# The down projection of batches 1 to 3 as seven block products per pair of chunks

## The chip, the cores and the metric

The kernel runs on one core of one Trainium2 chip. The time is the device time of one execution in microseconds (us). Before the change it is 421.93 us, the median of 3 runs (421.92 to 422.65).

## The reference

Two layers, each added to its input x (4 batches, 512 tokens, 256 features, all float32). The first mixes eight 256x256 weight matrices by eight numbers per batch and applies the mix. The second is a mixture of gated MLPs (256 to 1024 to 256): of eight experts each batch uses the two with the largest softmax weight, and one shared MLP is used by every batch.

```python
def _gemma_mlp(x, gate_w, up_w, down_w):
    g = jnp.einsum('bsh,hi->bsi', x, gate_w)
    u = jnp.einsum('bsh,hi->bsi', x, up_w)
    return jnp.einsum('bsi,ih->bsh', jax.nn.gelu(g, approximate=True) * u, down_w)
...
    masked_w = weight * mask[None, :, :]
    w_bot = jnp.einsum('bg,got->bot', y, masked_w)
    return jnp.einsum('bnt,bot->bno', x, w_bot) + bias
...
x = x + _L0_cond_ref(x, cond_8, L0_cond_weight, L0_cond_mask, L0_cond_bias)
x = x + _L1_cond_ref(x, cond_8, L1_cond_skill_gate, L1_cond_skill_up, L1_cond_skill_down, L1_cond_shared_gate, L1_cond_shared_up, L1_cond_shared_down)
```

## The kernel before

Everything lies feature-major: 128 features on the partitions, the 512 tokens of one batch (T) along the free axis, so the 256 features are two halves (HH). The batches go one after the other; batches 0 to 2 are one loop on every engine, batch 3 (the last) is written out. A batch is 24 **steps**. A step is one chunk of 128 of the 1024 inner features of one MLP: steps 0 to 7 are the shared MLP, 8 to 15 and 16 to 23 the two routed experts.

Each float32 operand is split into a high and a low part of type fp32r (`_hi`, `_lo`), and a product is three matmuls: hi by hi, hi by lo, lo by hi. A step is therefore 12 matmuls for gate and up (`gate_up`, L296 to L328: two projections, two input halves, three parts) and 6 for down (`down`, L330 to L345: two output halves, three parts), each of 128x128 weights over 512 columns. The down products of all 24 steps of a batch add up in one PSUM tile `o_ps`. TensorE's order at step s is `gate_up(s + 2)`, then `down(s)`, and once per batch, at step 13, the 12 matmuls of the next batch's first layer. `g_ps` and `u_ps` have two banks each and change places every step.

The other engines work on one step's data after the other:

- ScalarE: `gelu` from `g_ps` (L444), the high parts of one chunk of routed weights (`ex_hi`, L453, 768 columns: gate, up and down), the high part of h (`h_hi`, L456).
- VectorE: h = gelu times up, times the routing weight in routed steps (`form_h`, L614 to L624, written over `u_ps`), then the low part (`split_h`, L629, reads `u_ps` in PSUM and `h_hi` in SBUF). Between them stand the mixing of the next batch's first-layer weights (L584 to L596) and the low parts of the next batch's input (`x_lo`, L600).
- GpSimd: the low part of one chunk of routed weights per step (`ex_lo`, L721, 768 columns, both inputs in SBUF), in 16 of a batch's 24 steps.
- SyncE starts the loads: one chunk of weights is 384 KB (`raw`).

The order on each engine is written out by hand; engines wait for one another by counted semaphores (`g_done`, `gelu_done`, `h_done`, `h_hi_done`, `h_lo_done`, `w_lo_done`, `down_done`).

Of the kernel before, what the change touches and what calls it, by code (L numbers as in the profile page):

```python
# [22 lines left out]
WARM_UP = 5
L0_STEP = 13


def build(nc, xT, cond, l0_w, l0_mask, experts, shared, outT):
    B, _, HH, T = xT.shape
    G = l0_w.shape[0]
    E, CHUNKS, _, WC = experts.shape  # L30
# [13 lines left out]

    assert RAW_SLOTS == CHUNKS == RING and STEPS % 2 == 0 and STEPS % H_SLOTS == 0 and G == E == 8 and FIRST + SPLIT_LEAD + 1 == CHUNKS

    with ExitStack() as ctx:
# [78 lines left out]
        raw_in = [sem(f"raw_in{i}") for i in range(RAW_SLOTS)]  # L128
# [656 lines left out]
```

## Time and profile before

| | |
|---|---|
| median of 3 runs | 421.93 us (421.92 to 422.65) |
| the profiled execution, its own time | 422.23 us |
| its span (first to last instruction) | 420.1 us |
| TensorE busy (matmul) | 415.3 us, 99% |
| VectorE busy | 189.7 us, 45% |
| ScalarE busy | 184.7 us, 44% |
| GpSimd busy | 140.3 us, 33% |
| TensorE clock granted | 0.999 of full speed |

The page counts for each engine the time in which an instruction runs. Around the span lie 2.1 us of the profiled execution's own time.

### The profile page before, as it was taken

To read this page: it belongs to the slowest core of one execution; us is meant where nothing else is said; L and a number is where in the kernel's file an instruction comes from. 1 tells how busy PE (TensorE), PEld (TensorE's weight loads), DVE (VectorE), ACT (ScalarE), POOL (GpSimd) and SP (SyncE) were. 2 spreads that over 40 slices of the span, in tenths; PEclk is the share of its full clock that TensorE was granted. 3 is DMA by queue.
4 is the path that set the end of the run, shared out by engine and by line. 5 is a ranking of instruction groups with operands and counts; after the bars stand their busy time and mean duration, and the time that the engine had idled before them with its cause. 6 is when DMAs were issued, how large, how long until landed. Compare 5 with 4: busy or idle time off the path is not lost.

```text
span 420.1 us, 5339 instructions
## 1 busy us (share of the span) xinstructions
PE 415.3 (99%) x1827; PEld 342.5 (82%) x1827; DVE 189.7 (45%) x300; ACT 184.7 (44%) x306; POOL 140.3 (33%) x86
## 2 busy tenths in 40 slices
PE   8999999999999999999999999999999999999997
PEld 6778888888888888888888888888888888888886
DVE  3567744353345455444344545524434433333434
ACT  5676454453324545345232554534422445354421
POOL 1566535343001354535100335443300053444500
PEclk9999999999999999999999999999999999999999
DMA  7964332312011323223102132322300123210001
GB/s 272 352 196 158 100 109 79 114 62 89 0 51 49 101 87 107 81 75 111 39 0 101 37 112 75 112 79 71 112 0 0 51 75 113 76 37 0 2 0 50
DMA packets 14849, 35.05 MB, mean 83 GB/s; under 512 B 1650, under 2 KB 3186, under 8 KB 14834
## 3 DMA queue, kind: packets, MB, share of 16 engines
q1 hardware_dynamic: 14544, 34.61, 24.9%
q10 hardware_dynamic: 290, 0.26, 0.2%
q8 instruction: 7, 0.11, 0.1%
q14 instruction: 8, 0.07, 0.0%
HBM read 32.77 MB, written 2.10 MB: 83 GB/s over the span
## 4 chain that ended last, share of the span: by engine, by line
PE 96%; DMA 1%; DVE 1%; SPq 1%; issue 0%; ACT 0%; DVEq 0%
PE o_ps L342 30%; PE g_ps L321 21%; PE u_ps L321 21%; PE u_ps L327 10%; PE g_ps L327 10%; DMA l_raw<-l_w 1%; PE l_ps L286 1%; PE l_ps L291 1%; PE l_ps L270 0%; DVE l_first L560 0%; PE l_ps L357 0%; SPq L188 0%; DVE out_sb L653 0%; PE l_ps L274 0%; SPq L176 0%
## 5 line engine op out<-in xcount | busy, mean ns | idle before, releaser
L721 POOL TENSOR_TENSOR ex_lo<-raw,ex_hi 128x768 fp32r<-128x768 f32 x64 | 123.4, 1929 | 240.7 <-ACT ex_hi L453 240.7
L444 ACT ACTIVATE gelu<-g_ps 128x512 f32<-128x512 f32 x96 | 57.4, 598 | 175.6 <-PE g_ps L327 175.4
L624 DVE SCALAR_TENSOR_TENSOR u_ps<-gelu,route_cur,u_ps 128x512 f32<-128x512 f32 x64 | 48.3, 755 | 125.5 <-ACT gelu L444 125.5
L629 DVE TENSOR_TENSOR h_lo<-u_ps,h_hi 128x512 fp32r<-128x512 f32 x96 | 66.3, 691 | 31.6 <-ACT h_hi L456 30.5
L456 ACT CAST h_hi<-u_ps 128x512 fp32r<-128x512 f32 x96 | 56.4, 588 | 37.1 <-DVE u_ps L619 18.5
L453 ACT CAST ex_hi<-raw 128x768 fp32r<-128x768 f32 x64 | 52.9, 826 | 0.0
L321 PE MATMUL g_ps<-x_hi,ex_hi 128*128 (+1 forms) x128 | 49.8, 389 | 0.0
L321 PE MATMUL g_ps<-x_hi,ex_lo 128*128 (+1 forms) x128 | 49.8, 389 | 0.0
L321 PE MATMUL u_ps<-x_hi,ex_hi 128*128 (+1 forms) x128 | 49.8, 389 | 0.0
L321 PE MATMUL u_ps<-x_hi,ex_lo 128*128 (+1 forms) x128 | 49.8, 389 | 0.0
L342 PE MATMUL o_ps<-h_hi,ex_hi 128*128 128x512 f32 x122 | 47.5, 389 | 0.0
L342 PE MATMUL o_ps<-h_lo,ex_hi 128*128 128x512 f32 x122 | 47.5, 389 | 0.0
L342 PE MATMUL o_ps<-h_hi,ex_lo 128*128 128x512 f32 x122 | 47.5, 389 | 0.0
L619 DVE TENSOR_TENSOR u_ps<-gelu,u_ps 128x512 f32<-128x512 f32 x32 | 22.2, 695 | 43.7 <-ACT gelu L444 43.7
L327 PE MATMUL u_ps<-x_lo,ex_hi 128*128 (+1 forms) x128 | 39.4, 389 | 0.0
L327 PE MATMUL g_ps<-x_lo,ex_hi 128*128 (+1 forms) x128 | 39.4, 389 | 0.0
L321 PEld LDWEIGHTS g_ps<-x_hi,ex_hi 128*128 128x128 f32 x128 | 24.0, 188 | 5.0
L321 PEld LDWEIGHTS u_ps<-x_hi,ex_lo 128*128 128x128 f32 x128 | 24.0, 188 | 5.0
L327 PEld LDWEIGHTS g_ps<-x_lo,ex_hi 128*128 128x128 f32 x128 | 24.0, 188 | 5.0
L321 PEld LDWEIGHTS u_ps<-x_hi,ex_hi 128*128 128x128 f32 x128 | 24.0, 188 | 5.0
L321 PEld LDWEIGHTS g_ps<-x_hi,ex_lo 128*128 128x128 f32 x128 | 24.0, 188 | 5.0
L327 PEld LDWEIGHTS u_ps<-x_lo,ex_hi 128*128 128x128 f32 x128 | 24.0, 188 | 5.0
(119 smaller groups left out, 561.6 us busy)
## 6 DMA issues: line engine op xcount, KB each, us to landing
raw<-experts SPq DMA_DIRECT2D x64, 384.0 KB, 2.9
raw<-shared SPq DMA_DIRECT2D x8, 384.0 KB, 8.2
l_raw<-l_w SPq DMA_DIRECT2D x8, 256.0 KB, 6.0
x_in<-xT SPq DMA_DIRECT2D x8, 256.0 KB, 4.3
outT<-out_sb SPq DMA_DIRECT2D x8, 128.0 KB, 2.0
outT<-out_sb SPq DMA_DIRECT2D x3, 256.0 KB, 2.1
mask<-l_mask SPq DMA_DIRECT2D x2, 128.5 KB, 6.2
outT<-out_sb ACTq DMA_DIRECT2D x2, 128.0 KB, 2.0
```

The lines of the kernel that those rows point to most:

```text
L286: pe.matmul(l0_ps[:, oh], w[:, at:at + P], x_hi[:, th], start=(th == 0 and w is l0_hi), stop=False)
L291: mm = pe.matmul(l0_ps[:, oh], l0_hi[:, at:at + P], x_lo[:, th], start=False, stop=(th == HH - 1))
L321: pe.matmul(ps, w[:, at:at + P], x1_at(x1_hi, b, hh), start=(hh == 0 and w is w_hi), stop=False)
L327: mm = pe.matmul(ps, w_hi[:, at:at + P], x1_at(x1_lo, b, hh), start=False, stop=(hh == HH - 1))
L342: mm = pe.matmul(o_ps[:, oh], w[:, at:at + P], x[:, s % H_SLOTS], start=(s == 0 and i == 0), stop=((closes or s == STEPS - 1) and i == 2))
L444: act.activation(gelu[:, s % 2], g_ps[:, s % 2], ACT.Gelu_apprx_tanh).then_inc(gelu_done, 1)
L453: act.copy(ex_hi[:, j % RING], raw[:, j % RAW_SLOTS]).then_inc(w_hi_done, 1)
L456: act.copy(h_hi[:, s % H_SLOTS], u_ps[:, s % 2]).then_inc(h_hi_done, 1)
L619: dve.tensor_tensor(u_ps[:, s % 2], gelu[:, s % 2], u_ps[:, s % 2], ALU.mult).then_inc(h_done, 1)
L624: dve.scalar_tensor_tensor(u_ps[:, s % 2], gelu[:, s % 2], route_cur[:, k:k + 1], u_ps[:, s % 2], ALU.mult, ALU.mult).then_inc(h_done, 1)
L629: dve.tensor_tensor(h_lo[:, s % H_SLOTS], u_ps[:, s % 2], h_hi[:, s % H_SLOTS].bitcast(F32), ALU.subtract).then_inc(h_lo_done, 1)
L721: pool.tensor_tensor(lo, raw[:, slot], hi.bitcast(F32), ALU.subtract).then_inc(w_lo_done, 1)
```

## The change

The down projection of two chunks (a **pair**, steps 2p and 2p+1) is a product of 2 by 2 blocks: two output halves by two chunks of weights, times two chunks by two halves of the tokens (256 columns, TH). After the change it is done with seven block products in place of eight, as P1 to P7, in 34 pairs: all 12 of batches 1 and 2, and the first 10 of batch 3 (`fast(b, p)`). Batch 0 and the last two pairs of batch 3 stay as they were; batch 0 is now written out too, and batches 1 and 2 are the loop.

- TensorE: a fast pair is 21 matmuls over 256 columns, `products_123` (9) at the even step and `products_4567` (12) at the odd one, in place of 12 over 512. They add up over a batch in seven quarters and halves of banks. `g_ps` is one bank now, the other holds P1, P6 and P7; so the gate matmuls of step s+1 wait until the gelu of step s has read it, and all six gate matmuls stand ahead of the six for up.
- VectorE, per fast pair: the even step's h goes to `h_a` in SBUF (`form_a`); T1 to T4, sums and differences of token halves of the two chunks, are four instructions of 256 columns (`form_t1`, `form_t234`); their low parts are one of 1024 columns (`split_t`), in the next pair's even step; the low parts of h itself are `split_b11` (256 columns, from `h_a`) and `split_b2` (512, from `u_ps`). In the odd steps 7 to 21 of fast pairs VectorE forms S1 to S4 of the next pair but one's routed weights, four instructions of 128x128 (`expert_s`).
- ScalarE: one copy of 1024 columns more per fast pair (`split_t`, high parts), 384 + 512 columns of down weights (`split_d`) and 512 of gate and up per step (`split_gu`) in place of 768.
- GpSimd: the same widths for the low parts. It forms the shared S1 to S4 once, late in batch 0 (`shared_s`, from down weights loaded a second time), and takes the low parts of the next batch's input from VectorE (`split_x`, `split_x1`). Behind batches 1 and 2 it puts the products together with x (`sum_products`, five additions); ScalarE copies the products out of PSUM first, and VectorE adds P4. In batch 3 VectorE adds the products.
- Loads: gate and up (256 KB) and down (128 KB) come apart, in rings of four and two.

```diff
+A11, A12, A22, A21, S1, S2, S3, S4 = 0, 1, 2, 3, 3, 4, 5, 6
+B11, B21, B22, T1, T3, T2, T4 = 0, 1, 2, 3, 4, 5, 6
...
+        h_hi = sb("h_hi", [P, 7 * TH], F32R)
+        h_lo = sb("h_lo", [P, 7 * TH], F32R)
+        t_raw = sb("t_raw", [P, 4 * TH])
+        h_a = sb("h_a", [P, T])
...
-        g_ps = psum("g_ps", [P, 2, T])
...
+        g_ps = psum("g_ps", [P, T])[:]
...
+        P1, P6, P7 = p_ps[:, 0, 0:TH], p_ps[:, 1, 0:TH], p_ps[:, 1, TH:T]
+        P2, P3, P4, P5 = o_ps[:, 0, 0:TH], o_ps[:, 0, TH:T], o_ps[:, 1, 0:TH], o_ps[:, 1, TH:T]
...
+        def fast(b, p):
+            return not at_first(b) and not (at_last(b) and p >= LAST_FAST)
...
+                pe.wait_ge(gelu_done, n)
+                project(g_ps, w_hi, w_lo, GATE, b).then_inc(g_done, 1)
...
+            def product(ps, wt, ht, blk, hf, first, last):
+                for i, (w, h) in enumerate(((0, 0), (0, 1), (1, 0))):
+                    mm = pe.matmul(ps, block_of(wt[w], blk), half_of((h_hi, h_lo)[h], hf), start=(first and i == 0), stop=(last and i == 2))
...
+            def products_123(b, p):
+                wait_d(b, p)
+                pe.wait_ge(h_lo_done, STEPS * b + 2 * p + 2)
...
+                product(P1, wt, None, A11, B11, first, last)
+                product(P2, wt, None, A12, B21, first, False)
+                product(P3, wt, None, S4, B22, False, last).then_inc(down_done, 1)
...
+            def products_4567(b, p):
+                pe.wait_ge(t_lo_done, pair_count(b, p) + 1)
...
+                product(P6, wt, None, S2, T2, first, False)
+                product(P7, wt, None, S3, T3, False, last)
+                product(P4, wt, None, A22, T4, first, False)
+                product(P5, wt, None, S1, T1, False, last).then_inc(down_done, 1)
...
+                if fast(b, PAIRS + q):
+                    act.copy(ed_hi[:, q % RING_D, 0:3 * P], raw_d[:, slot, 0:3 * P]).then_inc(d_hi_done, 1)
+                    act.wait_ge(s_raw_done, 4 * s_count(b, q) + 4)
+                    act.copy(ed_hi[:, q % RING_D, S1 * P:7 * P], s_raw[:]).then_inc(s_hi_done, 1)
...
+            def split_t(b, p):
+                act.wait_ge(t_done, 4 * pair_count(b, p) + 4)
+                act.wait_ge(down_done, STEPS * b + 2 * p)
+                act.copy(h_hi[:, T1 * TH:7 * TH], t_raw[:]).then_inc(t_hi_done, 1)
...
+            def form_t1(b, p):
+                if not (isinstance(b, int) and b == 1 and p == 0):
+                    dve.wait_ge(t_lo_done, pair_count(b, p))
+                dve.wait_ge(h_done, STEPS * b + 2 * p + 1)
+                dve.tensor_tensor(t_part(T1), h_a[:, TH:T], h_a[:, 0:TH], ALU.subtract).then_inc(t_done, 1)
...
+            def form_t234(b, p):
+                dve.tensor_tensor(t_part(T3), u_ps[:, 1, TH:T], h_a[:, TH:T], ALU.subtract).then_inc(t_done, 1)
+                dve.wait_ge(t_done, 4 * pair_count(b, p) + 1)
+                dve.tensor_tensor(t_part(T2), u_ps[:, 1, TH:T], t_part(T1), ALU.subtract).then_inc(t_done, 1)
+                dve.wait_ge(t_done, 4 * pair_count(b, p) + 3)
+                dve.tensor_tensor(t_part(T4), u_ps[:, 1, 0:TH], t_part(T2), ALU.subtract).then_inc(t_done, 1)
...
+            def split_b11(b, p):
+                dve.wait_ge(h_hi_done, STEPS * b + 2 * p + 1)
+                dve.tensor_tensor(h_lo[:, 0:TH], h_a[:, 0:TH], h_hi[:, 0:TH].bitcast(F32), ALU.subtract).then_inc(h_lo_done, 1)
...
+            def split_b2(b, p):
+                dve.wait_ge(h_hi_done, STEPS * b + 2 * p + 2)
+                at = slice(B21 * TH, (B22 + 1) * TH)
+                dve.tensor_tensor(h_lo[:, at], u_ps[:, 1], h_hi[:, at].bitcast(F32), ALU.subtract).then_inc(h_lo_done, 1)
...
+            def split_t(b, p):
+                dve.wait_ge(t_hi_done, pair_count(b, p) + 1)
+                at = slice(T1 * TH, 7 * TH)
+                dve.tensor_tensor(h_lo[:, at], t_raw[:], h_hi[:, at].bitcast(F32), ALU.subtract).then_inc(t_lo_done, 1)
...
+            def expert_s(b, q):
...
+                dve.tensor_tensor(out(S1), blk(A21), blk(A22), ALU.add).then_inc(s_raw_done, 1)
+                dve.tensor_tensor(out(S3), blk(A11), blk(A21), ALU.subtract).then_inc(s_raw_done, 1)
+                dve.wait_ge(s_raw_done, n + 1)
+                dve.tensor_tensor(out(S2), out(S1), blk(A11), ALU.subtract).then_inc(s_raw_done, 1)
+                dve.wait_ge(s_raw_done, n + 3)
+                dve.tensor_tensor(out(S4), blk(A12), out(S2), ALU.subtract).then_inc(s_raw_done, 1)
...
+            def step(b, s, with_next):
+                p = s // 2
+                if not fast(b, p):
+                    form_h(b, s)
+                    if s % 2 == 0 and s > 0 and fast(b, p - 1):
+                        split_t(b, p - 1)
+                    beside(b, s, with_next)
+                    split_h(b, s)
+                elif s % 2 == 0:
+                    form_a(b, p)
+                    if p > 0 and fast(b, p - 1):
+                        split_t(b, p - 1)
+                    beside(b, s, with_next)
+                    form_t1(b, p)
+                    split_b11(b, p)
+                else:
                     form_h(b, s)
                     beside(b, s, with_next)
-                    split_h(b, s)
+                    split_b2(b, p)
+                    form_t234(b, p)
+                q = (s - CHUNKS + 1) // 2
+                if not at_first(b) and s % 2 and 0 <= q < EPR and fast(b, PAIRS + q):
+                    expert_s(b, q)
...
+            def split_d(b, q):
+                pool.wait_ge(d_hi_done, PAIRS + EPR * b + q + 1)
+                slot = d_slot(b, q)
+                if fast(b, PAIRS + q):
+                    pool.tensor_tensor(ed_lo[:, q % RING_D, 0:3 * P], raw_d[:, slot, 0:3 * P], ed_hi[:, q % RING_D, 0:3 * P].bitcast(F32), ALU.subtract)
+                    pool.wait_ge(s_hi_done, s_count(b, q) + 1)
+                    pool.tensor_tensor(ed_lo[:, q % RING_D, S1 * P:7 * P], s_raw[:], ed_hi[:, q % RING_D, S1 * P:7 * P].bitcast(F32), ALU.subtract).then_inc(d_lo_done, 1)
+                else:
+                    pool.tensor_tensor(ed_lo[:, q % RING_D, 0:W2], raw_d[:, slot], ed_hi[:, q % RING_D, 0:W2].bitcast(F32), ALU.subtract).then_inc(d_lo_done, 1)
...
+            def sum_products(b):
...
+                pool.tensor_tensor(out_flat, x1_all(b).rearrange("p (q c) -> p q c", c=TH), stage_1.unsqueeze(1).to_broadcast([P, 4, TH]), ALU.add).then_inc(sum_done, 1)
+                pool.wait_ge(sum_done, n + 1)
+                pool.tensor_tensor(out_flat[:, 1:4], out_flat[:, 1:4], stage_67[:, 0:TH].unsqueeze(1).to_broadcast([P, 3, TH]), ALU.add).then_inc(sum_done, 1)
```

What the order of the instructions shows, on the two engines of which the prediction speaks. In brackets stand the semaphores for which a row waits. First VectorE before, all that it does in step 11 of batches 1 and 2:

```order
L616 REGISTER_ALU
L624 SCALAR_TENSOR_TENSOR u_ps<-gelu,route_cur,u_ps 128x512 [waits u_done,gelu_done]
L599 REGISTER_ALU
L600 TENSOR_TENSOR x_lo<-x_in,x_hi 128x512 [waits x_hi_done]
L629 TENSOR_TENSOR h_lo<-u_ps,h_hi 128x512 [waits h_hi_done]
```

Then VectorE after the change, a pair of routed steps, 18 and 19 (`h_a` and `t_raw` lie in SBUF; `h_lo` is now one tile for the low parts of B11, B21, B22 and T1 to T4):

```order
L1007 SCALAR_TENSOR_TENSOR h_a<-gelu,route_cur,u_ps 128x512 [waits u_done,gelu_done]
L1037 TENSOR_TENSOR h_lo<-t_raw,h_hi 128x1024 [waits t_hi_done]
L1016 TENSOR_TENSOR t_raw<-h_a 128x256 [waits h_done,t_lo_done]
L1027 TENSOR_TENSOR h_lo<-h_a,h_hi 128x256 [waits h_hi_done]
L978 REGISTER_ALU
L986 SCALAR_TENSOR_TENSOR u_ps<-gelu,route_cur,u_ps 128x512 [waits u_done,gelu_done]
L1032 TENSOR_TENSOR h_lo<-u_ps,h_hi 128x512 [waits h_hi_done]
L1019 TENSOR_TENSOR t_raw<-u_ps,h_a 128x256
L1020 REGISTER_ALU
L1021 TENSOR_TENSOR t_raw<-u_ps,t_raw 128x256 [waits t_done]
L1022 REGISTER_ALU
L1023 TENSOR_TENSOR t_raw<-u_ps,t_raw 128x256 [waits t_done]
```

The two low parts of a pair are now three instructions, with `split_t` of the pair before (L1037) behind the even step's h; `form_t1` (L1016) waits until `split_t` is done, since it writes over T1. Where routed weights follow, VectorE goes on with these, here behind step 19 (`raw_d` and `s_raw` lie in SBUF):

```order
L1050 REGISTER_ALU [waits raw_d_in1]
L1053 TENSOR_TENSOR s_raw<-raw_d 128x128 [waits d_lo_done]
L1054 TENSOR_TENSOR s_raw<-raw_d 128x128
L1055 ISA
L1056 TENSOR_TENSOR s_raw<-s_raw,raw_d 128x128 [waits s_raw_done]
L1057 REGISTER_ALU
L1058 TENSOR_TENSOR s_raw<-raw_d,s_raw 128x128 [waits s_raw_done]
```

They stand ahead of the next even step's `form_a`, and none of them was on VectorE before. GpSimd after the change, an even routed step (16; at the odd step the last two rows stand alone; before, it was one L721 of 768 columns at each step):

```order
L1253 REGISTER_ALU
L1256 TENSOR_TENSOR ed_lo<-raw_d,ed_hi 128x384 [waits d_hi_done]
L1257 REGISTER_ALU
L1258 TENSOR_TENSOR ed_lo<-s_raw,ed_hi 128x512 [waits s_hi_done]
L1223 REGISTER_ALU
L1224 TENSOR_TENSOR eg_lo<-raw_g,eg_hi 128x512 [waits gu_hi_done]
```

The down weights and their sums are two instructions at even steps now, ahead of gate and up.

## Rows read from the trace of the kernel before

**Rows 1.** The page: busy time by engine; the chain that ended last, by engine.
```profile
PE 415.3 (99%) x1827; PEld 342.5 (82%) x1827; DVE 189.7 (45%) x300; ACT 184.7 (44%) x306; POOL 140.3 (33%) x86
...
PE 96%; DMA 1%; DVE 1%; SPq 1%; issue 0%; ACT 0%; DVEq 0%
```

**Rows 2.** That chain in order of time: start us, us, instructions.
```profile
25.15 1.36 PE o_ps L342 x6
...
29.23 1.36 PE o_ps L342 x6
...
125.79 1.36 PE o_ps L342 x6
```

**Rows 3.** Timeline of PE, end of the program: start us, us, instruction.
```profile
409.87 0.39 PE L321 MATMUL g_ps<-x_hi,ex_hi 128*128 128x512 f32 x1
...
412.59 0.28 PE L357 MATMUL l_ps<-h_hi,ex_hi 128*128 128x256 f32 x1
...
416.78 0.28 PE L357 MATMUL u_ps<-h_hi,ex_lo 128*128 128x256 f32 x1
```

**Rows 4.** Start of the loop: ScalarE's first gelu, PE's step 1.
```profile
18.99 0.60 ACT L444 ACTIVATE gelu<-g_ps 128x512 f32<-128x512 f32 x1 [0.23 <-PE g_ps L327]
...
19.25 0.39 PE L321 MATMUL g_ps<-x_hi,sh_hi 128*128 128x512 f32 x1
```

**Rows 5.** Groups of VectorE by line and form: busy us, mean ns, idle before.
```profile
L629 DVE TENSOR_TENSOR h_lo<-u_ps,h_hi 128x512 fp32r<-128x512 f32 x96 | 66.3, 691 | 31.6 <-ACT h_hi L456 30.5
L624 DVE SCALAR_TENSOR_TENSOR u_ps<-gelu,route_cur,u_ps 128x512 f32<-128x512 f32 x64 | 48.3, 755 | 125.5 <-ACT gelu L444 125.5
L600 DVE TENSOR_TENSOR x_lo<-x_in,x_hi 128x512 fp32r<-128x512 f32 x8 | 5.5, 685 | 0.0
L653 DVE TENSOR_TENSOR out_sb<-out_sb,l_ps 128x256 f32<-128x256 f32 x2 | 0.8, 422 | 1.0 <-PE l_ps L357 1.0
```

**Rows 6.** Groups of ScalarE by line and form.
```profile
L407 ACT CAST x_hi<-x_in 128x512 fp32r<-128x512 f32 x8 | 5.0, 621 | 1.4 <-DMA x_in<-xT 1.4
L453 ACT CAST ex_hi<-raw 128x768 fp32r<-128x768 f32 x64 | 52.9, 826 | 0.0
L427 ACT CAST sh_hi<-raw 128x256 fp32r<-128x256 f32 x9 | 3.1, 401 | 0.0
```

**Rows 7.** A group of GpSimd by line and form.
```profile
L725 POOL TENSOR_TENSOR sh_lo<-raw,sh_hi 128x256 fp32r<-128x256 f32 x6 | 4.3, 739 | 13.5 <-ACT sh_hi L427 13.5
```

**Rows 8.** Timeline, VectorE and GpSimd, at 35 and 42 us.
```profile
35.17 1.87 POOL L721 TENSOR_TENSOR ex_lo<-raw,ex_hi 128x768 fp32r<-128x768 f32 x1
35.31 1.75 DVE L534 TENSOR_TENSOR pair_sum<-probs 128x4 f32<-128x4 f32 x1
...
42.45 1.84 POOL L721 TENSOR_TENSOR ex_lo<-raw,ex_hi 128x768 fp32r<-128x768 f32 x1 [2.23 <-ACT ex_hi L453]
42.49 1.82 DVE L544 SCALAR_TENSOR_TENSOR route_w<-pair,pair_rest 128x8 f32<-128x8 f32 x1
```

**Rows 9.** Timeline, VectorE and GpSimd, 239 to 241 us and 263 to 265 us.
```profile
239.65 1.86 POOL L721 TENSOR_TENSOR ex_lo<-raw,ex_hi 128x768 fp32r<-128x768 f32 x1 [2.23 <-ACT ex_hi L453]
...
240.23 0.69 DVE L629 TENSOR_TENSOR h_lo<-u_ps,h_hi 128x512 fp32r<-128x512 f32 x1
...
263.36 0.75 DVE L624 SCALAR_TENSOR_TENSOR u_ps<-gelu,route_cur,u_ps 128x512 f32<-128x512 f32 x1 [1.98 <-ACT gelu L444]
264.03 0.69 DVE L600 TENSOR_TENSOR x_lo<-x_in,x_hi 128x512 fp32r<-128x512 f32 x1
264.13 2.29 POOL L721 TENSOR_TENSOR ex_lo<-raw,ex_hi 128x768 fp32r<-128x768 f32 x1 [2.24 <-ACT ex_hi L453]
```

**Rows 10.** Timeline of one late step: hand-offs between ScalarE and VectorE.
```profile
408.25 0.60 ACT L444 ACTIVATE gelu<-g_ps 128x512 f32<-128x512 f32 x1 [2.07 <-PE g_ps L327]
408.88 0.75 DVE L624 SCALAR_TENSOR_TENSOR u_ps<-gelu,route_cur,u_ps 128x512 f32<-128x512 f32 x1 [1.98 <-ACT gelu L444]
...
409.67 0.59 ACT L456 CAST h_hi<-u_ps 128x512 fp32r<-128x512 f32 x1 [0.82 <-DVE u_ps L624]
```

More of the change, by code:

```diff
@@ L322, in gate_up @@
[L322 to L330 removed]
+                    pe.wait_ge(gu_lo_done, gu_index(b, s - CHUNKS) + 1)
@@ L394, in _ @@
             first_layer_0()
-            for s in range(LAG):
-                gate_up(0, s)
-            with pe.Fori(0, B - 1) as b:
+            first_gate_up()
+            gate_up(0, 1)
+            batch(0, True)
+            with pe.Fori(1, B - 1) as b:
                 batch(b, True)
@@ new lines, in next_beside @@
+            def next_beside(b, s):
+                if s in (8, 10):
+                    split_x(b + 1, (s - 8) // 2)
+                if s == 11:
+                    split_l0(b + 1)
+                if s in (17, 21):
+                    split_x1(b + 1, (s - 17) // 4)
+            def step(b, s, with_next):
+                activate(b, s)
+                if s % 2 == 0 and s > 0 and fast(b, s // 2 - 1):
+                    split_t(b, s // 2 - 1)
+                weights_beside(b, s)
+                if not fast(b, s // 2):
+                    split_h(b, s)
+                elif s % 2 == 0:
+                    split_b11(b, s // 2)
+                else:
+                    split_b2(b, s // 2)
+                if with_next:
+                    next_beside(b, s)
@@ new lines, in batch @@
+            def batch(b, with_next):
+                for s in range(2, STEPS):
+                    step(b, s, with_next)
+                if with_next:
+                    activate(b + 1, 0)
+                    if not at_first(b):
+                        split_t(b, NP - 1)
+                    split_b11(b + 1, 0)
+                    if not at_first(b):
+                        evacuate_123(b)
+                    activate(b + 1, 1)
+                    split_b2(b + 1, 0)
+                    if not at_first(b):
+                        evacuate_4567(b)
@@ L707, in _ @@
             route_index()
-            form_h(0, 0)
-            split_h(0, 0)
+            for s in range(2):
+                step(0, s, False)
             batch(0, True)
@@ L736, in _ @@
             for c in range(FIRST):
[L737 to L745 removed]
+                split_gate(c)
@@ L747 @@
+                split_up(c)
+            split_shared_d(0)
+            for i in range(1, PAIRS):
+                for c in range(2 * i + 1, min(2 * i + 3, CHUNKS)):
+                    split_shared(c)
+                if i < PAIRS - 1:
+                    split_shared_d(i)
+            batch_0()
+            with pool.Fori(1, B - 1) as b:
+                batch(b, True)
+            batch(B - 1, False)
 def kernel(**inputs):
```

851 lines of the change are left out of this document (605 added, 246 removed).

## The prediction

> **What bounds the kernel now.** I read the page first: TensorE is busy 99% of the span and 96% of the chain that ended last; no other engine passes 45% [rows 1]. The reader is to see that a share of busy time so near to 100 leaves nothing to gain by making another engine faster. The chain in order of time says the same from within: the down products of one step start 4.08 us after those of the step before, and after one batch the same place comes 100.64 us later, which is 24 steps of 4.08 and the 2.72 of the first layer [rows 2]. PE's timeline has the price of a matmul: 12 of 512 columns from 409.87 to 412.59, 0.2267 us each, so a step is 18 of them, with no gap; and 35 of 256 columns from 412.59 to 416.78, 0.1197 each [rows 3]. Elsewhere the trace shows every chain of one step (gelu, h, high part, low part) [rows 10] waiting for TensorE's matmuls, not the reverse. So the time falls by what TensorE gives up, unless another engine then needs longer than TensorE for a pair of steps. That is the question here: the change gives TensorE a little less, and VectorE much more.
>
> **What TensorE gives up.** A fast pair has 21 matmuls of 256 columns in place of 12 of 512: 21 x 0.1197 = 2.514 against 12 x 0.2267 = 2.720, 0.206 less [rows 3]. That is far from the eighth that seven products for eight suggests, since 256 columns cost 53% of 512. Over 34 pairs: -7.0 us. The Trainium skill ("TensorE: Matmul & The Clock Gate", section "Back-to-back issue gap") puts a matmul of N columns at its stream time, N/2.4 ns, and some 2.5 ns; by that the pair would save 0.296, all pairs 10.1. The rows show 13 ns in place of 2.5 at both widths, so I go by the rows, and keep the page's figure as a small rival. A pair then takes TensorE 24 x 0.2267 + 2.514 = 7.95.
>
> **The edges.** With one bank for `g_ps`, the gate matmuls of step 1 wait for the first gelu, which ends at 19.59; they began at 19.25 [rows 4]: +0.35 to +0.4, once, since later the gelu lies far ahead of the bank's next use. At the change from batch 0 to 1 the first `products_123` waits for two additions of 512 columns that stand on VectorE behind other work: 0 to 0.3, I take 0.1. Together +0.5. The products' evacuations, the separate loads and ScalarE's wider copies lie beside TensorE's work: ScalarE was busy 44% [rows 1], and gains about 1.05 (1024 columns) and some 0.5 per pair of 7.95. If that cover were gone it would show as the waits worked out next.
>
> **What VectorE and GpSimd do to each other.** Both fetch from SBUF. At 42.45 GpSimd starts a 768-column split of 1.84; VectorE's instruction on 8 columns, at 42.49, takes 1.82 and ends with it; one on 4 columns at 35.31 takes 1.75 and ends 0.02 behind GpSimd's [rows 8]. The other way round, VectorE's `x_lo` of 264.03 to 264.72 stands ahead of a GpSimd split that starts at 264.13 and takes 2.29, 0.45 more than 1.84; but a `split_h`, which reads one operand from PSUM, runs its plain 0.69 in the midst of such a split [rows 9]. So a VectorE instruction with both inputs in SBUF and a GpSimd instruction don't run together here; the one that starts later waits for the other's end. The Trainium skill ("SBUF — State Buffer", section "Who interferes with whom") has the same rule, that the two engines hold a common port for a whole instruction; by that, and the trace agrees, it speaks against the change. Before, such VectorE instructions were the eight `x_lo` [rows 5] and small ones. After, a pair has three: `split_t` (1024 columns), `form_t1` and `split_b11` (256), and where routed weights follow four sums of 128, beside four GpSimd splits.
>
> **Prices.** VectorE: 512 columns 0.685, 256 columns 0.42 [rows 5]; in a straight line 1024 is 1.21 and 128 is 0.29; one behind the other they start some 0.07 before the last ends (0.08 from the instruction of 263.36 to the next [rows 9]). ScalarE: 512 columns 0.62, 768 0.83, 256 0.40 [rows 6], so 384 is 0.51 and 1024 1.05. GpSimd: 256 columns 0.74 [rows 7], 768 1.84 [rows 8], so 384 is 1.02, 512 1.29, 1024 2.40. Hand-offs: 0.04 from VectorE to ScalarE [rows 10], I take 0.03 back and 0.07 to GpSimd.
>
> **One routed pair, from its odd step's `form_h` at t = 0.** h 0 to 0.75; ScalarE's high part to 1.38; `split_b2` to 2.10; T3, T2, T4 to 3.30; S1 to S4 to 4.31; the next even step's `form_a` 4.25 to 5.0. Meanwhile ScalarE takes T's high parts 3.34 to 4.39 and the 384 columns to 4.80, so GpSimd starts its 384 split at 4.87, to 5.84. `split_t` could start at 4.92: it is **0.05 us too late** and waits, 5.87 to 6.95. `form_t1` waits by semaphore for `split_t`'s completion, and GpSimd's 512 split of the sums, ready since 5.4, is there first: 6.9 to 8.15. `form_t1` runs 8.18 to 8.5, `split_b11` directly behind, and the next odd `form_h` starts at 8.85. TensorE needs 7.95: the pair comes 0.9 late. With no contention the last number is 6.9, so VectorE's own work fits (1.05 of slack); the whole loss is two GpSimd splits met on the way. What is queued behind: `form_t1` holds `split_b11` and the odd `form_h`, TensorE waits for both.
>
> TensorE's wait begins when a slack is used up: `split_t`'s result is needed at 7.74 of the same count and there at 6.99, 0.75. Each of batches 1 and 2 has 8 pairs with sums, of which 7 follow another: 7 x 0.9 - 0.75 = 5.55. Batch 3 has 6: 5 x 0.9 - 0.75 = 3.75. Sum +14.85. In shared pairs (two splits per pair, no sums) VectorE keeps up.
>
> At the start of batches 2 and 3 GpSimd runs `sum_products`: 2.40 + 1.84 + 3 x 1.29 = 8.1 us almost in one piece, against which the first pair's `split_t` and `form_t1` stand. I make them 1.7 late (one 768 or 512 addition each, less the slack); the four shared pairs give back about half, 0.95 stays: +1.9. Bounds: 0, if VectorE gets in between two additions, and twice 3.5.
>
> **Sum, against the profiled execution's 422.23.** -7.0 + 0.5 + 14.85 + 1.9 = +10.3: 432.5; from the median of the runs shown, 0.3 lower, 421.93 + 10.3 = **432.2**. Its own range: the 0.9 between 0.6 and 1.25 (a 512 split's whole length) and the batch starts within their bounds give 427 to 439.
>
> **Rivals.** (1) Faster, the other side: **`split_t` starts before GpSimd's 384 split.** Then VectorE has 4.92 to 6.14, GpSimd 6.0 to 6.97, `form_t1` comes to 7.3 and `split_b11` to 7.65; the next form_h at 7.6 is within 7.95 and nothing stalls in the routed pairs: -7.0 + 0.5 = 415.4. It decides at 0.05 us of the count above, whose terms are each good to some 0.05; for it speaks that VectorE runs ahead of ScalarE whenever a pair is late, against it the two rows in which VectorE, 0.04 and 0.14 behind, was the one that waited [rows 8].
> (2) Much slower: **GpSimd also gets in between `form_t1` and `split_b11`**, or ahead of the sums, one more 512 split per pair: 10.05 in place of 8.85. The stalls are 7 x 2.1 - 0.75 = 13.95 twice and 5 x 2.1 - 0.75 = 9.75, with the batch starts and the other terms +33: 455. Shared pairs would take 8.65, 0.7 late in 12 of them, up to 463; at every second routed pair alone it is about half-way from the forecast, 444. For it: GpSimd has one more split ready at that point; against it: `split_b11` waits for nothing, so it stands directly behind.
> (3) Mixed: the order falls now one way, now the other, since a late pair moves ScalarE's copies as well: 418 to 428, between (1) and the forecast.
> (4) The page's 2.5 ns: no stalls and -10.1, 412.3.
> That the products don't save at all would need 256 columns at 0.1295 or more; 35 in a row showed 0.1197 [rows 3].
>
> **Numbers.** Chances: forecast 0.42, (1) 0.30, (2) 0.13, (3) 0.12, (4) 0.03. (1) has an error of some 2 us of its own (the edges, 0 to 0.9; a few pairs that are late all the same). So the range reaches from 413.5 to 444.0, the lower edge of (2); out are (4), about a tenth of (1), and most of (2), near 2 in 10. Within 0.2% (0.85 us, about what a measurement of this kernel can tell) lies a thin strip of (3), 0.04; faster are (1), (4) and some of (3), 0.38; slower the forecast, (2) and the rest of (3), 0.58.
>
> **What the changed kernel's profile would show.** Matmuls of 256 columns 0.12 apart within a group (L563), and TensorE's share of the chain far below 96%. Waits of PE on VectorE, at the products and named after `t_lo_done` and `h_lo_done`, growing within the routed steps of batches 1 to 3, none in batch 0. `split_t` (L1037) and `form_t1` (L1016) of twice their price or more, ending together with a GpSimd split (L1256, L1258), in nearly all routed pairs; a routed pair of 8.85, a shared one of 7.95. A gap of 0.4 at 19.6. At the start of batches 2 and 3 VectorE's instructions end with those of L1307 to L1314. Wrong it is if `split_t` shows its plain 1.2 (rival 1: the order at that point), if `split_b11` is long too (rival 2), or if ScalarE's copies, priced by lines through two rows, turn out to be what VectorE waits for.

## The result: 435.1 us, 3.1% slower

The changed kernel takes 435.1 us (median of 4 runs, 434.66 to 435.4) against 421.95; the ratio is 1.0307, with a 95% interval of 1.0289 to 1.0325. The page of the profile after has, where [rows 1] stood:

```profile
PE 416.8 (96%) x2133; PEld 348.0 (80%) x2133; DVE 334.6 (77%) x547; ACT 223.1 (52%) x407; POOL 240.6 (56%) x183
...
PE 53%; DVE 29%; issue 11%; ACT 4%; DMA 1%; DVEq 1%; SPq 1%; ACTq 0%
```

TensorE's busy share fell by little, from 99 to 96%, but its share of the chain that ended last went from 96 to 53%, and VectorE took 29%. A busy share alone would not have shown that another engine sets the pace. VectorE's 334.6 us "busy" hold waiting too, as its groups by line show (busy us, mean ns of one):

```profile
L1037 DVE TENSOR_TENSOR h_lo<-t_raw,h_hi 128x1024 fp32r<-128x1024 f32 x34 | 49.7, 1461 | 2.8 <-ACT h_hi L764 2.8
L1027 DVE TENSOR_TENSOR h_lo<-h_a,h_hi 128x256 fp32r<-128x256 f32 x34 | 44.7, 1316 | 0.6 <-ACT h_hi L754 0.6
L1016 DVE TENSOR_TENSOR t_raw<-h_a 128x256 f32<-128x256 f32 x34 | 32.9, 966 | 0.6
...
L1023 DVE TENSOR_TENSOR t_raw<-u_ps,t_raw 128x256 f32<-128x256 f32 x34 | 14.4, 425 | 1.2
```

All of the last three lines write 256 columns. The one that reads `u_ps` in PSUM takes 0.43; `form_t1` (L1016) and `split_b11` (L1027), both inputs in SBUF, take 0.97 and 1.32. Where the extra goes is seen in the timeline of one routed pair, VectorE and GpSimd (start us, us), with the odd `form_h` (L986) of this pair and the two before it:

```profile
166.84 0.74 DVE L986 SCALAR_TENSOR_TENSOR u_ps<-gelu,route_cur,u_ps 128x512 f32<-128x512 f32 x1
...
176.51 0.74 DVE L986 SCALAR_TENSOR_TENSOR u_ps<-gelu,route_cur,u_ps 128x512 f32<-128x512 f32 x1
...
180.63 0.75 DVE L1007 SCALAR_TENSOR_TENSOR h_a<-gelu,route_cur,u_ps 128x512 f32<-128x512 f32 x1
...
181.29 1.22 DVE L1037 TENSOR_TENSOR h_lo<-t_raw,h_hi 128x1024 fp32r<-128x1024 f32 x1
181.30 2.09 POOL L1256 TENSOR_TENSOR ed_lo<-raw_d,ed_hi 128x384 fp32r<-128x384 f32 x1 [3.56 <-ACT ed_hi L720]
...
182.54 1.13 DVE L1016 TENSOR_TENSOR t_raw<-h_a 128x256 f32<-128x256 f32 x1
...
183.35 1.47 POOL L1258 TENSOR_TENSOR ed_lo<-s_raw,ed_hi 128x512 fp32r<-128x512 f32 x1
183.59 1.50 DVE L1027 TENSOR_TENSOR h_lo<-h_a,h_hi 128x256 fp32r<-128x256 f32 x1
184.78 2.72 POOL L1224 TENSOR_TENSOR eg_lo<-raw_g,eg_hi 128x512 fp32r<-128x512 f32 x2
185.02 0.74 DVE L986 SCALAR_TENSOR_TENSOR u_ps<-gelu,route_cur,u_ps 128x512 f32<-128x512 f32 x1
```

The reader is to see two queues taking turns. `split_t` was there 0.01 us before GpSimd's 384 split and runs its plain 1.22; the split, worth 1.02, takes 2.09, for it waited. `form_t1` then ends 0.28 after that split, `split_b11` 0.27 after the next one (183.35 + 1.47 = 184.82), although it was queued directly behind `form_t1`: GpSimd's waiting instruction went in between. The next odd `form_h` starts at 185.02; the one before it stands at 176.51, so this pair took 8.51.

TensorE's waits in the view of waits (us in total, times, longest):

```profile
PE p_ps L563 <- DVE h_lo L1032: 6.7, 15, 1.6
PE p_ps L563 <- DVE h_lo L1037: 4.2, 5, 1.6
...
PE g_ps L502 <- ACT gelu L740: 0.3, 1, 0.3
```

To see in which stretch they lie, take the first product of a batch, of its first routed pair (in batch 1 also of the pair before it and of the next three), and of the next batch, from PE's timeline:

```profile
126.32 0.38 PE L563 MATMUL p_ps<-h_hi,sd_hi 128*128 128x256 f32 x1
...
150.91 0.35 PE L563 MATMUL p_ps<-h_hi,sd_hi 128*128 128x256 f32 x1
...
160.57 0.35 PE L563 MATMUL p_ps<-h_hi,ed_hi 128*128 128x256 f32 x1 [0.53 <-DVE h_lo L1032]
...
169.07 0.36 PE L563 MATMUL p_ps<-h_hi,ed_hi 128*128 128x256 f32 x1 [0.25 <-DVE h_lo L1032]
...
178.75 0.36 PE L563 MATMUL p_ps<-h_hi,ed_hi 128*128 128x256 f32 x1 [0.53 <-DVE h_lo L1032]
...
188.20 0.28 PE L563 MATMUL p_ps<-h_hi,ed_hi 128*128 128x256 f32 x1
...
229.77 0.28 PE L563 MATMUL p_ps<-h_hi,sd_hi 128*128 128x256 f32 x1
...
267.69 0.36 PE L563 MATMUL p_ps<-h_hi,ed_hi 128*128 128x256 f32 x1 [0.53 <-DVE h_lo L1032]
267.88 0.28 PE L563 MATMUL p_ps<-h_lo,ed_hi 128*128 128x256 f32 x1
...
336.89 0.28 PE L563 MATMUL p_ps<-h_hi,sd_hi 128*128 128x256 f32 x1
...
371.36 0.36 PE L563 MATMUL p_ps<-h_hi,ed_hi 128*128 128x256 f32 x1 [0.21 <-DVE h_lo L1032]
...
417.48 0.28 PE L563 MATMUL p_ps<-h_hi,ed_hi 128*128 128x256 f32 x1
```

So the four shared pairs of batches 1, 2 and 3 took 34.25, 37.92 and 34.47, and the eight routed pairs of batches 1 and 2 (with the first layer) 69.20 each; from 371.36 to the last fast product step at 417.48 it is 46.12. In batch 1 the loss is not spread evenly: the three routed pairs from 160.57 to 188.20 took 27.63, of which 1.36 is half of the first layer, and the five behind them, with the other half, 41.57. The same stretches are read from every run below, in this order: shared 1, 2, 3; routed 1, 2, 3. They leave out what lies ahead of batch 1: its first product came at 126.32 here and between 124.93 and 126.41 in the runs of its variants below. That difference arises in the first 20 us of an execution, which no edit below is meant to change.

### The profile page after: what moved, and what is told of

It reads as the page before. It is cut to its first block, busy times and chain, and to the rows that moved or that the text cites. A ratio compares the mean times of both kernels' runs of the same rounds, so it can differ in the third digit from the quotient of the medians.

```text
span 433.2 us, 6965 instructions
## 1 busy us (share of the span) xinstructions
PE 416.8 (96%) x2133; PEld 348.0 (80%) x2133; DVE 334.6 (77%) x547; ACT 223.1 (52%) x407; POOL 240.6 (56%) x183
## 4 chain that ended last, share of the span: by engine, by line
PE 53%; DVE 29%; issue 11%; ACT 4%; DMA 1%; DVEq 1%; SPq 1%; ACTq 0%
PE o_ps L556 7%; DVE h_lo L1027 7%; PE g_ps L502 6%; PE g_ps L503 6%; PE g_ps L506 6%; PE u_ps L506 6%; PE u_ps L502 6%; PE u_ps L503 6%; PE o_ps L563 4%; DVE h_lo L1037 4%; PE p_ps L563 4%; DVE t_raw L1016 2%; DVE h_lo L1032 2%; ACT h_hi L759 2%; PE l_ps L461 2%
## 5 line engine op out<-in xcount | busy, mean ns | idle before, releaser
L1224 POOL TENSOR_TENSOR eg_lo<-raw_g,eg_hi 128x512 fp32r<-128x512 f32 x64 | 90.0, 1421 | 45.2 <-ACT eg_hi L711 45.2
L986 DVE SCALAR_TENSOR_TENSOR u_ps<-gelu,route_cur,u_ps 128x512 f32<-128x512 f32 x42 | 31.4, 748 | 33.5 <-PE u_ps L506 31.8
L1037 DVE TENSOR_TENSOR h_lo<-t_raw,h_hi 128x1024 fp32r<-128x1024 f32 x34 | 49.7, 1461 | 2.8 <-ACT h_hi L764 2.8
L503 PE MATMUL g_ps<-x_hi,eg_lo 128*128 128x512 f32 (+1 forms) x128 | 50.4, 394 | 0.0
L502 PE MATMUL g_ps<-x_hi,eg_hi 128*128 128x512 f32 (+1 forms) x128 | 50.1, 391 | 0.0
L502 PE MATMUL u_ps<-x_hi,eg_hi 128*128 128x512 f32 (+1 forms) x128 | 49.8, 389 | 0.0
L503 PE MATMUL u_ps<-x_hi,eg_lo 128*128 128x512 f32 (+1 forms) x128 | 49.8, 389 | 0.0
L1027 DVE TENSOR_TENSOR h_lo<-h_a,h_hi 128x256 fp32r<-128x256 f32 x34 | 44.7, 1316 | 0.6 <-ACT h_hi L754 0.6
L506 PE MATMUL g_ps<-x_lo,eg_hi 128*128 128x512 f32 (+1 forms) x128 | 39.6, 390 | 0.0
L506 PE MATMUL u_ps<-x_lo,eg_hi 128*128 128x512 f32 (+1 forms) x128 | 39.4, 389 | 0.0
L1032 DVE TENSOR_TENSOR h_lo<-u_ps,h_hi 128x512 fp32r<-128x512 f32 x34 | 23.5, 692 | 16.9 <-ACT h_hi L759 16.9
L1016 DVE TENSOR_TENSOR t_raw<-h_a 128x256 f32<-128x256 f32 x34 | 32.9, 966 | 0.6
```

Of the source, the lines that this page charges most:

```text
L502: pe.matmul(ps, w_hi[:, at:at + P], x1_at(x1_hi, b, hh), start=(hh == 0), stop=False)
L503: pe.matmul(ps, w_lo[:, at:at + P], x1_at(x1_hi, b, hh), start=False, stop=False)
L506: mm = pe.matmul(ps, w_hi[:, at:at + P], x1_at(x1_lo, b, hh), start=False, stop=(hh == HH - 1))
L1016: dve.tensor_tensor(t_part(T1), h_a[:, TH:T], h_a[:, 0:TH], ALU.subtract).then_inc(t_done, 1)
L1027: dve.tensor_tensor(h_lo[:, 0:TH], h_a[:, 0:TH], h_hi[:, 0:TH].bitcast(F32), ALU.subtract).then_inc(h_lo_done, 1)
L1037: dve.tensor_tensor(h_lo[:, at], t_raw[:], h_hi[:, at].bitcast(F32), ALU.subtract).then_inc(t_lo_done, 1)
```

## The experiments

**GpSimd's splits cut.** Batches 1 to 3, 2 columns in place of 512, 384 and 512.

```diff
-                pool.tensor_tensor(eg_lo[:, j % RING], raw_g[:, j % RAW_G], eg_hi[:, j % RING].bitcast(F32), ALU.subtract).then_inc(gu_lo_done, 1)
+                n = W2 if at_first(b) else 2
+                pool.tensor_tensor(eg_lo[:, j % RING, 0:n], raw_g[:, j % RAW_G, 0:n], eg_hi[:, j % RING, 0:n].bitcast(F32), ALU.subtract).then_inc(gu_lo_done, 1)
...
```

> GpSimd's splits of routed weights in batches 1 to 3 (gate and up, down, sums) work on 2 columns in place of 512, 384 and 512; their low parts are left stale. All waits, all work of the other engines and GpSimd's additions behind batches 1 and 2 stay. Theory (VectorE waits for GpSimd's running instruction): the stalls inside the batches go, 7.0 less and 0.5 more than before, and up to 3 from the additions stay: 415.5 to 418.5. Rival (VectorE's own longer list of work is too long for a pair of 7.95 us, whoever else runs): 428 or more. Rival (256-column products cost TensorE more than 0.1197): 419 to 425 with few waits of TensorE.

Measured: 421.16 us, ratio 0.9988 (0.9978 to 0.9998). Shared 32.10, 35.67, 32.97; routed 66.72, 66.72, 43.82. The routed stretches lost all of their waits: 66.72 is 8 x 8.00 and the 2.72 of the first layer. VectorE's instructions were the same ones, in the same order, so its own work fits; the rival of the too long list falls. The time lies above the expected range for two reasons: 4.6 us stay in the shared stretches of batches 2 and 3, where GpSimd's additions stand, and a pair takes 8.00 in place of 7.95. So the rival of dearer products holds in part, for 34 x 0.05 = 1.7.

**The sums on VectorE cut.** `dve.tensor_tensor(out(S1)[:, 0:2], blk(A21)[:, 0:2], blk(A22)[:, 0:2], ALU.add)`, and so the other three.

> VectorE's four sums S1 to S4 work on 2 columns in place of 128 (the rest of the sums stays stale). Theory: the sums themselves hardly wait, so routed pairs lose only their work, about 1 us of 8.5; TensorE's waits in routed pairs of some 8 us in all go, those in shared pairs and at the batch starts stay: 426 to 429. Rival (the sums are what GpSimd holds up): under 422, with split_t, form_t1 and split_b11 near their plain prices.

Measured: 427.59 us, ratio 1.0139 (1.0118 to 1.0159), within the theory's range, but only in part for its reason. `form_t1` and `split_b11` still take 0.95 and 1.32, so the sums are load and not the place of the waits. Shared 32.78, 36.46, 34.08; routed 68.63, 68.65, 44.25. In batch 3 most of the routed waits go, as expected (43.82 is the stretch without waits); in batches 1 and 2 only 0.6 of 2.5 goes. Of the 7.8 between the two profiled executions, 3.0 lie in routed stretches, 3.3 in shared ones and 1.4 ahead of batch 1; these last are not the sums'. The run cannot tell whether the load would matter without the waits; the last experiment does.

**The even step's h in PSUM.** One operand of `split_b11` and `form_t1` moves from SBUF to PSUM; ScalarE makes the copy `h_a`.

```diff
-                    dve.scalar_tensor_tensor(h_a[:], gelu[:, 0], route_cur[:, s // CHUNKS - 1:s // CHUNKS], u_ps[:, 0], ALU.mult, ALU.mult).then_inc(h_done, 1)
+                    dve.scalar_tensor_tensor(u_ps[:, 0], gelu[:, 0], route_cur[:, s // CHUNKS - 1:s // CHUNKS], u_ps[:, 0], ALU.mult, ALU.mult).then_inc(h_done, 1)
...
+                act.copy(h_a[:], u_ps[:, 0]).then_inc(a_done, 1)
...
-                dve.tensor_tensor(t_part(T1), h_a[:, TH:T], h_a[:, 0:TH], ALU.subtract).then_inc(t_done, 1)
+                dve.tensor_tensor(t_part(T1), u_ps[:, 0, TH:T], h_a[:, 0:TH], ALU.subtract).then_inc(t_done, 1)
...
-                dve.tensor_tensor(h_lo[:, 0:TH], h_a[:, 0:TH], h_hi[:, 0:TH].bitcast(F32), ALU.subtract).then_inc(h_lo_done, 1)
+                dve.tensor_tensor(h_lo[:, 0:TH], u_ps[:, 0, 0:TH], h_hi[:, 0:TH].bitcast(F32), ALU.subtract).then_inc(h_lo_done, 1)
```

`split_b11` now stands ahead of `form_t1`, both wait for the copy, and the next up projection waits for T1.

> The even step's h stays in PSUM; ScalarE copies it to h_a (512 columns more per pair), so split_b11 and form_t1 read one operand from PSUM. split_t and the sums still read SBUF alone. Theory: form_t1 and split_b11 come back to about 0.42 each, 1.4 us less per pair; a routed pair is then at most some 7.9 on VectorE, near TensorE's 7.95: 415.5 to 421. Rival (own work): ScalarE's copy lengthens the chain, 433 to 438.

Measured: 419.09 us, ratio 0.9928 (0.9911 to 0.9944): 0.7% below the kernel before. Shared 32.10, 34.17, 32.00; routed 66.72, 66.72, 43.82. VectorE's groups by line of this run (L1029 is `split_b11`, L1017 `form_t1`, L1039 `split_t`):

```profile
L1039 DVE TENSOR_TENSOR h_lo<-t_raw,h_hi 128x1024 fp32r<-128x1024 f32 x34 | 56.1, 1651 | 0.6 <-ACT h_hi L766 0.6
...
L1029 DVE TENSOR_TENSOR h_lo<-u_ps,h_hi 128x256 fp32r<-128x256 f32 x34 | 14.2, 416 | 3.4 <-ACT h_a L756 3.0
...
L1017 DVE TENSOR_TENSOR t_raw<-u_ps,h_a 128x256 f32<-128x256 f32 x34 | 14.0, 412 | 0.0
```

GpSimd's work is unchanged, and the two instructions came to 0.42 and 0.41. They also start later now, behind the copy, and in the other order; that they no longer wait for GpSimd is seen where one runs in the midst of a split:

```profile
177.11 1.30 POOL L1260 TENSOR_TENSOR ed_lo<-s_raw,ed_hi 128x512 fp32r<-128x512 f32 x1
177.22 0.41 DVE L1017 TENSOR_TENSOR t_raw<-u_ps,h_a 128x256 f32<-128x256 f32 x1
```

Both take their plain time. `split_t`, still with both in SBUF, waits a little more than before (1.65), and that fits beside TensorE's 8.00.

**GpSimd's splits in halves.** Each is two instructions of half the columns.

```diff
-                pool.tensor_tensor(eg_lo[:, j % RING], raw_g[:, j % RAW_G], eg_hi[:, j % RING].bitcast(F32), ALU.subtract).then_inc(gu_lo_done, 1)
+                for h in (slice(0, D), slice(D, W2)):
+                    mm = pool.tensor_tensor(eg_lo[:, j % RING, h], raw_g[:, j % RAW_G, h], eg_hi[:, j % RING, h].bitcast(F32), ALU.subtract)
+                mm.then_inc(gu_lo_done, 1)
...
```

> Each GpSimd split of batches 0 to 3's routed weights is two instructions of half the columns; same work, 4 more instructions per pair. Theory (VectorE waits for the one running instruction, then goes ahead of GpSimd's next): each of three waits per pair is at most 0.75 in place of 1.3: 423 to 430. Rival (once behind, VectorE waits for all that GpSimd has queued): as long as the changed kernel or longer, 434 to 440.

Measured: 424.18 us, ratio 1.0058 (1.0041 to 1.0074): 10.9 us less than the changed kernel by more instructions for the same work. `form_t1` takes 0.72 and `split_b11` 0.93. A VectorE instruction waits for the GpSimd instruction ahead of it, not for what is queued behind that.

**The additions behind batches 1 and 2 cut** (the last dimension of each to `0:2`, in the changed kernel).

> The changed kernel with GpSimd's five additions behind batches 1 and 2 on 2 columns per quarter (the rest of the outputs of these batches is left stale). Theory: the waits of the first two pairs of batches 2 and 3 behind these additions go, as large as the 4.4 that were left where GpSimd's splits were cut: 430 to 431.5. Rival (what is late at a batch's start is given back in its shared pairs): 433.5 to 435.

Measured: 428.62 us, ratio 1.0162 (1.0142 to 1.0183), 6.5 less than the changed kernel and more than expected. Shared 33.13, 34.85, 32.00; routed as in the changed kernel (69.22, 69.19, 46.11). Of the 6.5, 3.1 and 2.5 lie in the shared stretches of batches 2 and 3, where the additions run, so they cost 5.5 there, and nothing of it is given back. A further 1.1 lies in batch 1, ahead of any addition; why it differs there, no run shows. How the additions cost time is seen in the changed kernel's timeline at the start of batch 3 (VectorE and GpSimd):

```profile
336.77 2.40 POOL L1307 TENSOR_TENSOR out_sb<-x,x_in 128x1024 f32<-128x1024 f32 x1 [11.07 <-DVE x L1072]
...
337.80 2.46 DVE L1037 TENSOR_TENSOR h_lo<-t_raw,h_hi 128x1024 fp32r<-128x1024 f32 x1
...
339.25 2.72 POOL L1309 TENSOR_TENSOR out_sb<-out_sb,x_in 128x768 f32<-128x768 f32 x1
...
340.30 1.96 DVE L1016 TENSOR_TENSOR t_raw<-h_a 128x256 f32<-128x256 f32 x1
...
342.05 1.36 POOL L1311 TENSOR_TENSOR out_sb<-out_sb,x_in 128x512 f32<-128x512 f32 x1
342.18 1.51 DVE L1027 TENSOR_TENSOR h_lo<-h_a,h_hi 128x256 fp32r<-128x256 f32 x1
```

Each of the pair's three instructions waits for one addition of 1024, 768 or 512 columns: 1.2 + 1.5 + 1.1 late in this one pair.

**h in PSUM, and the additions late and in pieces.**

```diff
+                pool.wait_ge(t_lo_done, pair_count(b, NP - 1) + 1)
+                x1_q = x1_all(b).rearrange("p (q c) -> p q c", c=TH)
+                for q in range(4):
+                    mm = pool.tensor_tensor(out_flat[:, q], x1_q[:, q], stage_1, ALU.add)
+                mm.then_inc(sum_done, 1)
...
```

> As the kernel with the even step's h in PSUM, and GpSimd's additions are 13 of 256 columns that begin when split_t of the batch's last pair is done. Theory: that split_t is plain again, the copy behind it waits 0.7 at most, and the 2.0 of TensorE's waits at the start of batch 2 go: 417 to 418. Rival (the later additions only move the waits to the next pairs): 419 or more.

Measured: 417.93 us, ratio 0.991 (0.9894 to 0.9927). Shared 32.10, 33.06, 32.00: half of the loss at the start of batch 2 went, 1.1 stays. The later start and the smaller pieces were changed together; no run has one without the other.

**The kernel before with 256-column down products**, nothing else changed: no T, no S, no new waits.

```diff
-                    for i, (w, x) in enumerate(((w_hi, h_hi), (w_hi, h_lo), (w_lo, h_hi))):
-                        mm = pe.matmul(o_ps[:, oh], w[:, at:at + P], x[:, s % H_SLOTS], start=(s == 0 and i == 0), stop=((closes or s == STEPS - 1) and i == 2))
+                    for half in (slice(0, T // 2), slice(T // 2, T)):
+                        for i, (w, x) in enumerate(((w_hi, h_hi), (w_hi, h_lo), (w_lo, h_hi))):
+                            mm = pe.matmul(o_ps[:, oh, half], w[:, at:at + P], x[:, s % H_SLOTS, half], start=(s == 0 and i == 0 and half.start == 0), stop=((closes or s == STEPS - 1) and i == 2 and half.start > 0))
```

> The kernel before with each down matmul of 512 columns as two of 256, in batches 0 to 2 and the first 21 steps of batch 3, 93 steps; everything else is as it was. With 0.1197 per matmul of 256 columns a step grows by 12 x 0.1197 - 1.360 = 0.076: 429.0. Theory of a further cost (the six matmuls of 512 columns behind a row of 256-column ones take 0.027 longer): 431.5. Rival (the gate matmuls were slow for another reason, such as the one bank of g_ps): 428.7 to 429.3.

Measured: 431.16 us, ratio 1.0222 (1.02 to 1.0245). Over 93 steps that is 0.102 a step, the 0.076 of the products and 0.026 more. PE's timeline of this run, from the first matmul behind a row of products:

```profile
202.28 0.40 PE L321 MATMUL g_ps<-x_hi,ex_hi 128*128 x1
202.51 0.40 PE L321 MATMUL g_ps<-x_hi,ex_lo 128*128 x1
202.75 0.39 PE L321 MATMUL u_ps<-x_hi,ex_hi 128*128 x1
...
203.67 0.39 PE L321 MATMUL u_ps<-x_hi,ex_hi 128*128 x1
```

Six starts in 1.39 where six of 512 columns take 1.36 [rows 2], with gate and up in turn and two banks for `g_ps`. So it belongs to TensorE's row of narrow matmuls, not to the bank. Why these six are slower, no run shows.

**The sums on GpSimd**, in the changed kernel (`form_s` behind GpSimd's gate and up split of the odd step; VectorE's `expert_s` goes).

> The changed kernel with the four sums of routed weights on GpSimd (behind its gate and up split of the odd step) in place of VectorE. VectorE has 1.05 us less per routed pair, as in the run with the sums cut, GpSimd 4 x 0.465 = 1.9 more. Theory: the three waits of VectorE on GpSimd stay (they come from the splits, not from the sums), so routed pairs come to TensorE's 8.0 to 8.2 and 6 to 8 us go: 427 to 429. Rival (GpSimd then is late with the weights' low parts, or holds VectorE up once more per pair): 431 or more.

Measured: 427.06 us, ratio 1.0123 (1.0103 to 1.0143), about what cutting the sums gave. Shared 32.71, 35.93, 34.08; routed 69.07, 67.97, 44.24. The time is as expected, but only batch 3's routed pairs came close to TensorE's 8.00; in batches 1 and 2 they still lose 2.35 and 1.25. `form_t1` and `split_b11` still take 0.93 and 1.27.

**All three moves together**: h in PSUM, late additions, sums on GpSimd.

> The same move of the sums, on top of h in PSUM and the late additions. Theory: nothing waits for VectorE in routed pairs there any more, so the move buys nothing: 417.4 to 418.4, the same as without it. Rival (GpSimd's longer list delays split_t or the weights): 419 or more.

Measured: 416.87 us, ratio 0.9883 (0.9866 to 0.9899), the fastest of all, just under the expected range and some 1 us below the run without the move of the sums. By the stretches that 1 us is the start of batch 2 (33.06 there, 32.00 here); the two intervals just meet, so I don't claim more than that the move costs nothing here. Its page, and its products as above:

```profile
PE 409.4 (99%) x2133; PEld 350.6 (85%) x2133; DVE 271.0 (65%) x459; ACT 241.6 (58%) x441; POOL 273.4 (66%) x287
...
PE 96%; DMA 1%; DVE 1%; SPq 1%; issue 0%; ACT 0%; DVEq 0%
```
```profile
125.77 0.38 PE L564 MATMUL p_ps<-h_hi,sd_hi 128*128 128x256 f32 x1
...
157.86 0.28 PE L564 MATMUL p_ps<-h_hi,ed_hi 128*128 128x256 f32 x1
...
224.58 0.28 PE L564 MATMUL p_ps<-h_hi,sd_hi 128*128 128x256 f32 x1
...
256.58 0.28 PE L564 MATMUL p_ps<-h_hi,ed_hi 128*128 128x256 f32 x1
...
323.30 0.28 PE L564 MATMUL p_ps<-h_hi,sd_hi 128*128 128x256 f32 x1
...
355.30 0.28 PE L564 MATMUL p_ps<-h_hi,ed_hi 128*128 128x256 f32 x1
...
399.12 0.28 PE L564 MATMUL p_ps<-h_hi,ed_hi 128*128 128x256 f32 x1
```

Shared 32.09, 32.00, 32.00; routed 66.72, 66.72, 43.82: pairs of 8.00 throughout, and the 2.72 of the first layer in batches 1 and 2. TensorE is the chain again, as in [rows 1]. GpSimd is as busy as with the move of the sums alone, 273.4 us, more than in any other run, and does no harm: what counts is which VectorE instructions meet it.

## Why the prediction was right, and where it was lucky

The forecast was 432.2, within 427 to 439; measured were 435.1. The sign and its reason hold: TensorE gains a little and waits for VectorE, which waits for GpSimd. But two of the three signs by which the prediction said that it would be wrong came up: `split_t` shows its plain 1.2 in most routed pairs, and `split_b11` is long. The kind of wait was right; its place within the pair and its size in each stretch were not. Taken apart by the stretches, with the run of all three moves as the one without waits:

| term | forecast | measured | from |
|---|---|---|---|
| TensorE's own saving, 34 pairs | -7.0 | -5.4 | a pair of 8.00 against 8.16 |
| edges | +0.5 | about +0.8 | what is left of 13.15; 0.3 is the wait for the first gelu |
| routed pairs | +14.85 | +7.3 | 69.20 - 66.72 twice, 46.12 - 43.82 |
| shared stretches, with the batch starts | +1.9 | +10.5 | 34.25, 37.92, 34.47 against 32.09, 32.00, 32.00 |
| sum | +10.3 | +13.2 | |

- **The saving** was right in its spacing (0.12 within a row of products) and lacked the slow six behind each row: 2 x 0.027 of the 0.206 of every pair. In the changed kernel's timeline of PE, gates behind products and gates behind a plain step stand near the end (420.30 - 418.91 = 1.39, 424.38 - 423.02 = 1.36):

```profile
418.91 0.40 PE L502 MATMUL g_ps<-x_hi,eg_hi 128*128 128x512 f32 x1
...
420.30 0.39 PE L502 MATMUL u_ps<-x_hi,eg_hi 128*128 128x512 f32 x1
...
423.02 0.39 PE L502 MATMUL g_ps<-x_hi,eg_hi 128*128 128x512 f32 x1
...
424.38 0.39 PE L502 MATMUL u_ps<-x_hi,eg_hi 128*128 128x512 f32 x1
```

  The Trainium skill's figure of 2.5 ns per matmul ("TensorE: Matmul & The Clock Gate", section "Back-to-back issue gap", which gives it for the isolated gap of one matmul) would, as an estimate, have given -10.1; the rows of both kernels show 0.12 for 256 columns, and here the measurement decides.
- **The 0.05 us tie** was called the wrong way. `split_t` starts ahead of GpSimd's 384 split in 16 of the 22 routed pairs with sums, by 0.07 at most, and behind it in 6. But the step that failed in rival (1) is the other half of it: with `split_t` ahead, nothing was to stall. In fact `form_t1` met the 384 split and `split_b11` the 512 one.
- **"`split_b11` waits for nothing, so it stands directly behind"** was wrong, and it was the argument against rival (2). GpSimd's waiting instruction goes in between two VectorE instructions that stand back to back; that is half of rival (2)'s mechanism at one split's price, not on top of the forecast's order. The pair then takes 8.5 in place of 8.85.
- **The routed sum** left out two things that nearly cancel. With 8.5 and TensorE's 8.00, the forecast's own formula gives 7 x 0.5 - 0.75 = 2.75 for batch 1, near the measured 2.48, but not pair by pair: 2.27 of the 2.48 is lost in the first three routed pairs (27.63 - 1.36 - 3 x 8.00) and 0.21 in the other five. In those five VectorE's pairs take 8.51 all the same, but TensorE has the 2.72 of the first layer to do from step 13 on, a slack that the forecast didn't count. Ahead of that VectorE still has work for the next batch between its splits, and GpSimd the input's low parts (`split_x`, steps 9 and 11): the odd `form_h` of 166.84 and the next, at 176.51, stand 9.67 apart. Batch 3 has neither: its routed pairs stand 8.44 or 8.45 apart, and it loses 2.30.
- **"VectorE keeps up"**, said of the shared pairs, was wrong in batches 1 and 2. In most shared pairs `form_t1` and `split_b11` met the two gate and up splits, with the first-layer mixing of 0.75 per step between them, which I had not counted: with the additions cut, the shared stretches of batches 1 and 2 still lose 1.0 and 2.9. In batch 3, which mixes nothing, they lose nothing then. That comparison speaks for the mixing; no run cuts it alone. The largest part (160.57 - 150.91 = 9.66, so 1.66 of 2.16, in batch 1 of the changed kernel) lies in the last pair of the stretch, beside which VectorE and GpSimd do the first sums and down splits of the routed weights.
- **The batch starts** were undersized too: 5.5 by experiment against 1.9. I counted one wait each for `split_t` and `form_t1`, left `split_b11` out, and let the shared pairs give back half.

So the mechanism was right in kind, and the total came near by luck: a routed term twice too large stood against a shared one five times too small. The Trainium skill ("SBUF — State Buffer", section "Who interferes with whom") has the shared port as an exclusive lock; the runs with the splits cut and with h in PSUM agree (means of 0.55 and 0.48 for `form_t1` and `split_b11` in the first, 0.41 and 0.42 in the second, against 0.97 and 1.32).

## What to carry to other kernels

When work moves onto VectorE beside a busy GpSimd, count not its columns but the instructions that take both inputs from SBUF: each can wait for one whole GpSimd instruction, in turn. Leave one operand in PSUM where there is a copy engine to spare, cut the other engine's instructions shorter, or start its long ones later, in pieces, where VectorE reads PSUM. And before an algorithm with fewer multiplications is taken, price its narrower matmuls by the rows: here seven for eight was worth 2% of a pair, and only once nothing waited.

## What the hardware showed that was not expected

- Two engines' instructions with SBUF inputs take turns even where one engine's stand back to back (`split_b11` 1.50 behind `form_t1`, in place of 0.42, so 1.1 of it is waiting).
- Six 512-column matmuls behind a row of 256-column ones take 1.39 us in place of 1.36, with gate and up in turn over two banks of `g_ps` as with one.
- A wait costs TensorE 0.07 us or more beyond itself: behind one, the second product of the row starts 0.19 to 0.23 us after the first in place of 0.12 (267.69 to 267.88 in the changed kernel).
